# A wave-attention and mixture-of-experts layer on one core: routing's first chunk inside the last attention unit, pad rows in pairs, and a reordered wave projection with warm-up matmuls

## The chip, the cores and the metric

One NeuronCore of a Trainium2 chip runs the whole layer in one launch. The metric is the device time of one execution in microseconds, the median of several executions. The engines are PE (TensorE: matmuls and transposes), PEld (its weight loads), DVE (VectorE), ACT (ScalarE), POOL (GpSimd) and SP (SyncE, which here only issues transfers).

## The reference

The input is x of 4 x 1024 tokens with 256 channels, float32. Four steps follow each other.

```
wave:   wp = silu(x @ w_wave + b_wave)            -> freq, phase, decay (mean over 8 heads)
        q  = silu(x @ w_query + b_query)          -> score slope per head, q . key_weight
        33 sample positions per token, softmax, envelope, weighted sum of x at those positions
        gate (two small matmuls), @ w_out, silu;  x = layernorm(x + out)
msa:    x = x + softmax(q k^T / 4) v @ w_proj     (16 heads of 16, per batch of 1024 tokens)
moe:    z = layernorm(x) * w + b;  logits = z @ gate_w + gate_b;  expert = argmax (8 experts)
        x = layernorm(x + x2 + gelu(z @ w1[e]) @ w2[e])
```

The routing step sorts the 4096 tokens by expert into regions of a scratch tensor `routed`, so that the expert step can take them 128 rows at a time. Where an expert's region does not end on a multiple of 128, rows of zeros with an index beyond the last token fill it up (pad rows).

## The kernel before, in words

The program is a row of blocks. In a block every engine has its own list of instructions, the lists meet only in semaphores, and a barrier of all engines closes the block. Every list is written by hand; no scheduler moves anything.

- **constants** (L116 to L127): POOL makes the identity matrix `ident`, DVE casts it to `identb`. A block of its own, so its barrier stands before the first load.
- **project_waves** (L260 to L454): for each batch b of 1024 tokens, PE transposes x (`turn`, 16 transposes, `pw_pT`, L379), ACT and DVE copy the result to SBUF (`evacuate`, L338, L339, L426), PE multiplies it by the wave and query weights (`project`, `pw_pW`, L388), DVE adds the biases (`bias_add`, `pw_pre`, L410), ACT takes silu (`activate`, L346) and two tanh (`squash`), DVE sums query times key weight (`scores`, L416 and L421). Between these DVE works out the sampling grid of a batch: `locate`, `spots`, `within`, `counts`, `extremes` (L204 to L257). PE's `project` waits for all five loads on ACT's queue (`w_in`), and `project(b)` waits for `bias_add(b-1)`, since both use one PSUM tile. `activate(b)` waits for `qkd`, the end of `scores(b-1)`.
- **wave_sampling**, **gate_and_project**: not touched.
- **attention** (L1481 to L1763): 32 units of two heads, in 8 steps each. A step computes four score tiles (`at_pst`, L1714), ACT takes their exponential (L1616), PE multiplies the step before by v (`at_pacc`, L1724, `values`). The maxima of the next unit are computed in the same steps (`at_pmx`, L1695, three PSUM banks), so the last unit has none. After its last step PE transposes the sum back (`turn_out`, L1706), DVE normalises (L1655, L1661) and SP stores it (L1567). In that unit SP already loads routing's first chunk of the attention's result Y and of the residual y0 (L1595, L1596, tiles `first_y`, `first_y0`).
- **project_and_route** (L1781 to L2129): the tokens in chunks, seven of 512 and two of 256. `rounds()` runs three chunks at once: in round i PE does `project(i)` (L2092), `gate(i-2)` (L2125), `turn(i+1)` (L2083), `turn_n(i-1)` (L2102), `count(i-2)` (L2113 to L2116). ACT copies the transpose (`turn_out`, L1921, tile `pg_yT`), scales (L1928), takes the root (L1936) and normalises into `pg_rows` (L1944). DVE adds the residual (`add`, L2002), takes statistics (`spread`), picks expert and slot (`route_chunk`, `place_chunk`), and keeps the residual (`keep`, L2033). POOL scatters the rows, one indirect transfer for each 128 tokens (L1904). There is one buffer `yc` for Y: SP loads chunk i (L1845) once `turn(i-1)` is done, which is in round i-2; y0 has two buffers (L1848, after `keep(i-2)`). The eight pad transfers (L1840, 258 KB each) stand at i = 2. After the last chunk DVE works out the table of tiles (L2053 to L2070); SP waits for it, reads the first tile's expert, loads that expert's `w1` (L1852), waits for all scatters and loads the first tile's rows (L1857).
- **experts** (L2133 to L2295): 39 tiles of 128 rows, each 16 products with w1 (L2281), gelu, 8 products with w2 (L2291), and the last layernorm.

A float32 matmul stands as two records in the trace: 16 products are x32 there, 8 are x16. Transposes are one record each.

Of the kernel before, what the change touches and what calls it, by code (L numbers as in the profile page):

```python
# [11 lines left out]
P = 128  # L12
# [43 lines left out]
def build(nc, io, dr):  # L56

    with ExitStack() as top:
# [15 lines left out]
        constants(nc, sem, ident, identb)  # L74
# [3 lines left out]
        with ExitStack() as wave:  # L78
# [7 lines left out]
            with ExitStack() as ctx:  # L86
                project_waves(nc, sem, lambda *a: sb(ctx, *a), lambda *a: ps(ctx, *a), io, ident, grid)
# [7 lines left out]
        yn, y_out = [sb(top, f"at_yn{i}", [P, 8, 2, 2 * DK]) for i in range(2)], [sem(f"at_y_out{i}") for i in range(2)]  # L95
        with ExitStack() as both:
# [3 lines left out]
            with ExitStack() as ctx:  # L100
                attention(nc, sem, lambda *a: sb(ctx, *a), lambda *a: ps(ctx, *a), io, dr, ident, w2, w_in, proj_loads, projs_in,
                          first_in, first_loaded, yn, y_out, att)
# [3 lines left out]
        with ExitStack() as ctx:  # L106
            project_and_route(nc, sem, lambda *a: sb(ctx, *a), lambda *a: ps(ctx, *a), io, dr, ident, projs, projs_in, expert, at, first_in, first_loaded,
# [3 lines left out]


def constants(nc, sem, ident, identb):

    zeroed, made = sem("ident_zeroed"), sem("ident_made")
    with nc.Block() as block:  # L116
        @block.gpsimd
        def _(pool):
            nc.gpsimd.memset(ident[:], 0.0).then_inc(zeroed, 1)
            pool.wait_ge(zeroed, 1)  # L120
            nc.gpsimd.affine_select(out=ident[:], in_=ident[:], compare_op=ALU.not_equal, fill=1.0, base=0,
                                    pattern=[[-1, P]], channel_multiplier=1).then_inc(made, 1)

        @block.vector
        def _(dve):
            dve.wait_ge(made, 1)
            nc.vector.tensor_copy(identb[:], ident[:])  # L127
# [132 lines left out]
def project_waves(nc, sem, sb, ps, io, ident, grid):  # L260
# [13 lines left out]
    w_in, x_in = sem("wave_w_in"), [sem(f"wave_x_in{i}") for i in range(2)]  # L274
# [3 lines left out]
    MADE = 9  # L278
    biased, silued, tanhed, qprod, qkd = (sem("wave_" + n) for n in ("biased", "silued", "tanhed", "qk_products", "qk_summed"))
# [7 lines left out]
    with nc.Block() as block:  # L287
# [10 lines left out]
        def _(pool):  # L298
            g = nc.gpsimd
            near = ident[:, 0:2 * TILES].unsqueeze(1).to_broadcast([P, REACH, 2 * TILES])  # L300
# [14 lines left out]
            g.memset(grid.rows[:, grid.EDGE + L:2 * grid.EDGE + L], grid.OUTSIDE).then_inc(made, 1)  # L315
            pool.wait_ge(made, MADE - 1)
# [10 lines left out]
        def _(a):  # L327
            a.dma_start(w[:, :, 0:3 * WH], io["L0_attn_w_wave"].rearrange("(k p) n -> p k n", p=P)).then_inc(w_in, 16)
            a.dma_start(w[:, :, 3 * WH:NW], io["L0_attn_w_query"].rearrange("(k p) n -> p k n", p=P)).then_inc(w_in, 16)
            a.dma_start(bias[:, 0:3 * WH], row(io["L0_attn_b_wave"], 3 * WH)).then_inc(w_in, 16)  # L330
            a.dma_start(bias[:, 3 * WH:NW], row(io["L0_attn_b_query"], WH * POS)).then_inc(w_in, 16)
            a.dma_start(kw[:], row(io["L0_attn_key_weight"], POS)).then_inc(w_in, 16)
# [20 lines left out]

            nc.scalar.activation(warm[:, 0:1], ident[:, 0:1], ACT.Silu)
# [13 lines left out]
        def _(pe):  # L368
# [34 lines left out]
        def _(dve):  # L403
# [24 lines left out]
            c = Chain(dve, grid.nd)  # L428
            evacuate(0)
            dve.wait_ge(w_in, 5 * 16)  # L430
# [5 lines left out]
            dve.wait_ge(qkd, 1)  # L436
# [14 lines left out]
            bias_add(3)  # L451
            grid.extremes(v, c, 1)
# [545 lines left out]

# [1337 lines left out]
```

## Time and profile before

| | us |
|---|---|
| median of 3 runs | 1659.06 |
| lowest, highest | 1658.22, 1660.64 |
| profiled execution, its own time | 1656.7 |
| its span in the trace | 1654.9 |
| PE busy | 1539.9 (93%) |
| DVE busy | 1329.6 (80%) |
| ACT busy | 1012.4 (61%) |
| mean granted TensorE clock | 0.976 |

| stretch of the span, by its first and last work | us |
|---|---|
| constants and project_waves | 0.3 to 49.1 |
| wave_sampling, gate_and_project, attention | 49.6 to 1273.8 |
| project_and_route | 1274.4 to 1359.7 |
| experts | 1361.0 to the end |

The rows are read from one profiled execution. It took 1656.7 us, 1.8 more than its span and 2.4 less than the median of the three timed runs. A timeline row gives start, duration, engine, line, operation, output and input; equal instructions that follow each other stand in one row with their count. In square brackets is the time for which the engine stood idle ahead of it, and what ended that.

### The profile page before, as it was taken

What the parts mean: (1) busy time and instruction counts of PE and PEld (TensorE: products, weight loads), DVE (VectorE), ACT (ScalarE), POOL (GpSimd) and SP (SyncE); (2) the same over time, 40 slices, a digit from 0 to 9 for tenths busy, and PEclk for the clock granted to TensorE, in tenths of its full rate; (3) what the DMA queues carried; (4) which work ended last, traced back from release to release, by engine and by line L of the source; (5) the groups of instructions that cost most, each with busy time, mean ns of one, the idle gap of its engine ahead of it and who ended that gap; (6) DMA issues with size and microseconds to landing.
All of it is one profiled execution on the core that took longest, in us unless ns stands there. A gap on an engine that the chain in (4) does not pass through costs nothing. (4 is left out here: it accounts for less than half of the span.)

```text
span 1654.9 us, 29306 instructions
## 1 busy us (share of the span) xinstructions
PE 1539.9 (93%) x10078; PEld 837.9 (51%) x10078; DVE 1329.6 (80%) x3006; ACT 1012.4 (61%) x1745; POOL 196.0 (12%) x372
## 2 busy tenths in 40 slices
PE   7688999979998999999999999999997859999997
PEld 6465656656553222222222222222222858999996
DVE  5899999846888889888988898889880767777773
ACT  2599999935446777777777777777776532222221
POOL 3011111131110000000000000000000351222222
PEclk9799999999999999999999999999999979999999
DMA  3300110026847322232233222212202766666661
GB/s 108 89 8 14 50 43 21 14 96 218 265 167 197 71 59 55 69 71 54 51 70 71 60 52 71 72 49 56 71 21 81 218 223 236 209 211 210 204 203 54
DMA packets 159154, 172.22 MB, mean 104 GB/s; under 512 B 72912, under 2 KB 118992, under 8 KB 159008
## 3 DMA queue, kind: packets, MB, share of 16 engines
q1 hardware_dynamic: 153600, 156.60, 32.8%
q0 software_dynamic: 4432, 13.50, 2.1%
q8 instruction: 82, 1.34, 0.4%
q14 instruction: 64, 0.52, 0.1%
q10 hardware_dynamic: 976, 0.24, 0.1%
HBM read 120.73 MB, written 49.23 MB: 103 GB/s over the span
## 5 line engine op out<-in xcount | busy, mean ns | idle before, releaser
L1629 DVE TENSOR_REDUCE at_mx<-at_pmx 128x1 f32<-128x512 f32 x980 | 618.0, 681 | 57.8 <-PE at_pmx L1695 56.8
L1616 ACT ACTIVATE at_p<-at_pst 128x512 f32<-128x512 f32 x1024 | 533.2, 603 | 209.8 <-PE at_pst L1714 209.6
L1695 PE MATMUL at_pmx<-at_k,at_q 96*128 96x512 bf16 x980 | 374.7, 383 | 0.0
L1714 PE MATMUL at_pst<-at_q,at_k 99*128 99x512 bf16 x1024 | 346.6, 380 | 4.9 <-ACT at_p L1616 2.6
L1724 PE MATMUL at_pacc<-at_p,at_v 128*32 128x512 f32 x2048 | 272.8, 604 | 0.9 <-ACT at_p L1616 0.7
L1695 PEld LDWEIGHTS at_pmx<-at_k,at_q 96*128 96x128 bf16 x980 | 95.3, 97 | 239.1 <-DVE at_mx L1629 180.0
L1714 PEld LDWEIGHTS at_pst<-at_q,at_k 99*128 99x128 bf16 x1024 | 98.9, 98 | 156.7 <-ACT at_p L1616 92.2
L873 PE MATMUL ws_pA<-ident,ws_A 128*128 128x128 f32 x1088 | 148.6, 283 | 25.6 <-ACT ws_A L655 24.2
L2226 ACT ACTIVATE ex_hT<-ex_pH 128x1024 f32<-128x1024 f32 x39 | 39.9, 1024 | 202.4 <-PE ex_pH L2281 202.4
L873 PEld LDWEIGHTS ws_pA<-ident,ws_A 128*128 128x128 f32 x1088 | 119.8, 143 | 84.3 <-ACT ws_A L655 41.8
L2241 DVE STREAM_TRANSPOSE ex_zr<-ex_row 32x64 f32<-32x64 f32 x608 | 143.2, 235 | 17.9 <-DMA ex_row<-scratch_routed 10.0
L2281 PE MATMUL ex_pH<-ex_zT,ex_w 128*128 128x128 f32 x1248 | 147.8, 277 | 2.9 <-ACT ex_zT L2219 2.9
L2281 PEld LDWEIGHTS ex_pH<-ex_zT,ex_w 128*128 128x128 f32 x1248 | 147.3, 194 | 5.4 <-issue 3.4
L2291 PE MATMUL ex_pY<-w,ex_hT 128*128 x624 | 141.2, 379 | 0.7 <-DVE ex_x L2251 0.7
L2291 PEld LDWEIGHTS ex_pY<-w,ex_hT 128*128 128x128 f32 x624 | 115.6, 190 | 15.2 <-issue 1.1
L655 ACT ACTIVATE ws_A<-ws_steps,par_beta,par_alpha 128x672 f32<-128x672 bf16 (+2 forms) x128 | 100.0, 857 | 2.9 <-issue 2.3
L655 ACT ACTIVATE ws_A<-lent_steps,par_beta,par_alpha 128x672 f32<-128x672 bf16 (+2 forms) x128 | 100.2, 855 | 1.7 <-issue 1.7
L777 DVE TENSOR_TENSOR ws_AT<-ws_pA,ws_hitT 128x768 f32<-128x768 f32 (+2 forms) x96 | 89.8, 952 | 9.6 <-PE ws_pA L873 9.2
L777 DVE TENSOR_TENSOR ws_AT<-ws_pA,lent_hits 128x768 f32<-128x768 f32 (+2 forms) x96 | 90.4, 949 | 8.1 <-PE ws_pA L873 7.8
L1867 POOL MEMSET pg_eps<- 128x1 f32 x1 | 0.1, 104 | 783.4 <-POOLq L1510 783.4
L1724 PEld LDWEIGHTS at_pacc<-at_p,at_v 128*32 128x32 f32 x2048 | 40.8, 108 | 99.3 <-ACT at_p L1616 79.7
L1383 PE MATMUL gp_pQ<-gp_zT,gp_wqkv 128*128 128x512 f32 x128 | 60.9, 602 | 0.0
(271 smaller groups left out, 1568.7 us busy)
## 6 DMA issues: line engine op xcount, KB each, us to landing
ex_w<-in_L_ffn_w SPq DMA_DIRECT2D x39, 1024.0 KB, 5.4
at_q<-scratch_qs SPq DMA_DIRECT2D x192, 64.0 KB, 2.8
at_k<-scratch_ks SPq DMA_DIRECT2D x192, 64.0 KB, 2.9
ex_row<-scratch_routed SPq DMA_DIRECT2D x39, 258.0 KB, 5.0
scratch_v<-gp_v SPq DMA_DIRECT2D x8, 1024.0 KB, 6.9
at_v<-scratch_v SPq DMA_DIRECT2D x32, 256.0 KB, 3.7
w<-in_L_ffn_w SPq DMA_DIRECT2D x16, 512.0 KB, 4.6
scratch_qs<-gp_split SPq DMA_DIRECT2D x16, 384.0 KB, 3.2
```

The costliest lines, as they stand in the source:

```text
L655: nc.scalar.activation(A[:, h % QUAD, cols(g, r)], KB[g][:, cols(g, r)], ACT.Exp, bias=par["beta"][:, t, h], scale=par["alpha"][:, t, h]). ...
L777: v.tensor_tensor(AT[h // QUAD][:, home(h, m[0]):home(h, m[-1]) + 1, :].rearrange("p s l -> p (s l)"), p[:, 0:len(m) * P], mask, ALU.mult) ...
L873: last = nc.tensor.transpose(p[:, to], a, ident[:])
L1383: last = nc.tensor.matmul(pQ[q % 3][:], wqkv[:, k, q * P:(q + 1) * P], zT[:, k, :], start=(k == 0), stop=(k == KC - 1))
L1616: a.activation(pt[k // 2 % 4][:, k % 2, :], pst[bank(w, k)][:], ACT.Exp).then_inc(exped, 1)
L1629: v.reduce_max(mx[u % 2][:, m // 2, m % 2:m % 2 + 1], pmx[bank(w, m)][:], AX.X).then_inc(red, 1)
L1695: nc.tensor.matmul(pmx[bank(w, m)][:], qst[u][0:ROWS, h, nt * P:(nt + 1) * P], kst[u][0:ROWS, h, kh * HALF:(kh + 1) * HALF], start=True, s ...
L1714: nc.tensor.matmul(pst[bank(w, k)][:], kst[u][:, h, t * P:(t + 1) * P], qst[u][:, h, p * HALF:(p + 1) * HALF], start=True, stop=True).then ...
L1724: last = nc.tensor.matmul(pacc[at:at + 2 * DK, :], vst[u][:, s, h, :], pt[(2 * s + p) % 4][:, h, :], start=(s == 0), stop=(s == BT - 1))
L2241: last = v.transpose(zr[j % 2][c * Q:(c + 1) * Q, :, q * Q:(q + 1) * Q], z[q * Q:(q + 1) * Q, :, c * Q:(c + 1) * Q])
L2281: last = nc.tensor.matmul(pH[:, c, :], w1[j % WBUFS][:, k, c * P:(c + 1) * P], zT[:, k, :], start=(k == 0), stop=(k == KC - 1))
L2291: last = nc.tensor.matmul(pY[:], hT[j % 2][:, c, :], w2[:, c, bass.ds(e, 1), :], start=(c == 0), stop=(c == HC - 1))
```

## The change

It has five parts.

1. **The block of constants is gone.** POOL makes `ident` at the head of project_waves, and whoever reads it waits for a semaphore (`diagonal`). SP's and ACT's loads there wait for nothing.
2. **The wave projection is reordered.** `project` waits for the two weight loads alone; the biases and the key weight have a semaphore of their own, on which DVE waits. `bias_add(1)` stands ahead of `extremes(0)`, `bias_add(2)` ahead of `locate(1)`, and `activate(b)` waits for the products of `scores(b-1)` (`qprod`) only. PE gets nine matmuls ahead of the first transposes and seven between `turn(1)` and `turn(2)` (`unread`, 104 columns, written to columns of `pW` that nobody reads).
3. **Routing's chunk 0 moves into attention's last unit**: its transposes behind steps 1 to 4, its copies (DVE, two of 512 columns) behind DVE's last step, its projection behind steps 6 and 7 and around the last `values`, in the banks of the maxima. DVE adds the residual at the block's end. SP loads Y's chunk 1 there too. Routing starts with `turn(1)` and with an activation that loads ACT's table for the root.
4. **Pad rows in pairs**: two transfers after y0's load at i = 3, 4, 5 and 6, in place of eight at i = 2.
5. **w1 of the first tile is loaded without the table**: the table is made so that the first tile always belongs to expert 0 (one more DVE instruction), and SP loads `w1[0]` right after the last y0 load.

```diff
-        constants(nc, sem, ident, identb)
...
+            g.memset(ident[:], 0.0).then_inc(zeroed, 1)
+            pool.wait_ge(zeroed, 1)
+            g.affine_select(out=ident[:], in_=ident[:], compare_op=ALU.not_equal, fill=1.0, base=0,
+                            pattern=[[-1, P]], channel_multiplier=1).then_inc(diagonal, 1)
...
                 if b:
-                    a.wait_ge(qkd, b)
+                    a.wait_ge(qprod, b)
...
+            def unread(n):
+
+                for _ in range(n):
+                    nc.tensor.matmul(pW[:, 0, 0, NW:C], ident[:], ident[:, 0:C - NW], start=True, stop=True)
+
+            pe.wait_ge(diagonal, 1)
+            unread(WARMING)
             turn(0)
-            pe.wait_ge(w_in, 5 * 16)
+            pe.wait_ge(w_in, 2 * 16)
             project(0)
             turn(1)
+            pe.wait_ge(biased, 1)
+            unread(WAITING)
             turn(2)
...
             grid.counts(v, c, 0)
+            bias_add(1)
+            dve.wait_ge(qkd, 1)
             grid.extremes(v, c, 0)
-            bias_add(1)
             scores(1)
+            bias_add(2)
             dve.wait_ge(tanhed, 4)
             grid.locate(v, c, 1)
-            bias_add(2)
             scores(2)
...
+            sp.dma_start(first.yc[:], tokens(dr["Y"], 0)).then_inc(first.y_in, 16)
+            sp.dma_start(first.y0[:], tokens(dr["y0"], 0)).then_inc(first.y0_in[0], 16)
+            sp.wait_ge(first.turned, 1)
+            sp.dma_start(first.yc[:], tokens(dr["Y"], 1)).then_inc(first.y_in, 16)
...
             normalise(UNITS - 1, UNITS // RING - 1, RING - 1)
+            dve.wait_ge(first.outed, 1)
+            dve.wait_ge(first.y0_in[0], 16)
+            for n in range(2):
+                ins = v.tensor_tensor(first.x2[:, 2 * n:2 * n + 2, :], pO[n], first.y0[:, 2 * n:2 * n + 2, :], ALU.add)
+            ins.then_inc(first.added, 1)
...
+                    if final and TURNED <= s < TURNED + first.T:
+                        turn_first(s - TURNED)
+                    if final and s >= PROJECTED:
+                        project_first(s - PROJECTED)
...
             units(unit)
+            project_first(BT - PROJECTED)
             values(UNITS - 1, RING - 1, BT - 1)
+            project_first(BT - PROJECTED + 1)
...
-                if i == 2:
-                    sp.wait_ge(consts, CONSTS)
-                    for e in range(E):
-                        sp.dma_start(dr["routed"][e * REGION:e * REGION + P, :], padrow[:]).then_inc(pads_sent, 16)
...
+                if PADS <= i < PADS + E // 2:
+                    sp.wait_ge(consts, CONSTS)
+                    for e in range((i - PADS) * 2, (i - PADS) * 2 + 2):
+                        sp.dma_start(dr["routed"][e * REGION:e * REGION + P, :], padrow[:]).then_inc(pads_sent, 16)
...
+            sp.dma_start(w1[0][:], io["L0_ffn_w1"][0, :, :].rearrange("(k p) n -> p k n", p=P)).then_inc(w1_in[0], 16)
             sp.wait_ge(table, TABLE)
-            e = sp.value_load(expert[0:1, :], min_val=0, max_val=E - 1)
...
-            turn_out(0)
+            a.activation(warm[:], ident[:, 0:1], ACT.Sqrt)
...
-            turn(0)
             for i, prev, pp in rounds():
-                if i is not None:
+                if i:
                     project(i)
```

The order on PE at the end of attention and the head of routing, first of the kernel before. `at_pst` are score tiles, `at_pacc` the products with v, `at_pm` the transposes back, `pg_pY` and `pg_pO` routing's transposes and projection.

```order
L1714 MATMUL at_pst<-at_q,at_k 128x512 x4
L1724 MATMUL at_pacc<-at_p,at_v 32x512 x4
L1714 MATMUL at_pst<-at_q,at_k 128x512
L1724 MATMUL at_pacc<-at_p,at_v 32x512 x4
L1706 MATMUL at_pm<-ident,at_oe 128x128 x4
L1510 UNCONDITIONAL_BRANCH
L2073 UNCONDITIONAL_BRANCH
L2083 MATMUL pg_pY<-ident,first_y 128x128 x8
L2092 MATMUL pg_pO<-pg_wproj,pg_yT 128x256 x8
L2083 MATMUL pg_pY<-ident,first_y 128x128 x8
```

And of the kernel after, from step 6 of the last unit on. `at_pmx<-pg_wproj` is the projection of chunk 0.

```order
L1744 MATMUL at_pst<-at_q,at_k 128x512
L1772 MATMUL at_pmx<-pg_wproj,at_first_yT 128x256 x2
L1744 MATMUL at_pst<-at_q,at_k 128x512 x3
L1754 MATMUL at_pacc<-at_p,at_v 32x512 x4
L1744 MATMUL at_pst<-at_q,at_k 128x512
L1772 MATMUL at_pmx<-pg_wproj,at_first_yT 128x256 x4
L1754 MATMUL at_pacc<-at_p,at_v 32x512 x4
L1772 MATMUL at_pmx<-pg_wproj,at_first_yT 128x256 x2
L1736 MATMUL at_pm<-ident,at_oe 128x128 x4
L1526 UNCONDITIONAL_BRANCH
L2135 UNCONDITIONAL_BRANCH
L2145 MATMUL pg_pY<-ident,first_y 128x128 x8
```

Eight products of the projection now stand between score tiles and around the last product with v; behind the barrier only `turn(1)` is left of what stood ahead of `project(1)`.

SP's transfers at the head of routing, before:

```order
L1845 DMA first_y<-scratch_Y 128x4x256
L1848 DMA pg_y<-scratch_y 128x4x256
L1840 DMA scratch_routed<-pg_padrow 128x516 x8
L1845 DMA first_y<-scratch_Y 128x4x256
L1848 DMA first_y<-scratch_y 128x4x256
```

And after:

```order
L1902 DMA first_y<-scratch_Y 128x4x256
L1905 DMA pg_y<-scratch_y 128x4x256
L1909 DMA scratch_routed<-pg_padrow 128x516 x2
L1902 DMA first_y<-scratch_Y 128x4x256
L1905 DMA first_y<-scratch_y 128x4x256
L1909 DMA scratch_routed<-pg_padrow 128x516 x2
L1902 DMA first_y<-scratch_Y 128x4x256
```

The eight pad transfers no longer stand ahead of chunk 2's load; each of chunks 4 to 7 has a pair ahead of its load.

## Rows read from the trace of the kernel before

**Rows 1.** Timeline of project_waves: start us, us, engine, line, operation.

```profile
0.80 0.21 POOL L119 MEMSET ident<- 128x128 f32 x1 [0.29 <-POOLq L2325]
...
2.06 0.45 SPq L290 DMA_DIRECT2D pw_x<-in_L_attn_x  x1
...
11.65 6.05 PE L388 MATMUL pw_pW<-pw_w,pw_xT 128*128 128x152 f32 x32 [1.41 <-DVE pw_xT L426]
...
17.81 1.43 DVE L410 TENSOR_TENSOR pw_pre<-pw_pW,pw_bias 128x1216 f32<-128x1216 f32 x1 [6.31 <-PE pw_pW L388]
...
21.53 3.30 PE L379 MATMUL pw_pT<-ident,pw_x 128*128 128x128 f32 x16 [2.09 <-ACT pw_xT L339]
...
29.11 1.91 PE L379 MATMUL pw_pT<-ident,pw_x 128*128 128x128 f32 x16
...
30.85 4.34 PE L388 MATMUL pw_pW<-pw_w,pw_xT 128*128 128x152 f32 x32
...
32.02 1.23 DVE L416 TENSOR_TENSOR pw_prod<-pw_act,pw_kw 128x1024 f32<-128x1024 f32 x1 [1.28 <-ACT pw_act L346]
...
47.91 1.22 DVE L421 TENSOR_REDUCE ws_A<-pw_prod 128x64 f32<-128x1024 f32 x1
```

**Rows 2.** Windows: us, busy PE, PEld, DVE, ACT, POOL, PEclk, DMA share, GB/s.

```profile
27.61:29.31 1.70, 1.70 (x15) 1.70 (x15) 1.59 (x9) 0.00 (x0) 0.00 (x0) 1.00 0.00 0
...
1305.00:1309.00 4.00, 4.00 (x36) 3.92 (x35) 3.06 (x9) 2.13 (x5) 3.39 (x3) 1.00 0.48 144
1309.00:1313.00 4.00, 4.00 (x33) 3.59 (x31) 3.79 (x17) 3.14 (x7) 2.27 (x3) 1.00 1.03 302
```

**Rows 3.** Timeline of PE in attention's last unit, its last steps.

```profile
1267.21 0.39 PE L1714 MATMUL at_pst<-at_q,at_k 99*128 99x512 bf16 x1 [0.26 <-ACT at_p L1616]
...
1269.61 1.06 PE L1724 MATMUL at_pacc<-at_p,at_v 128*32 128x512 f32 x8 [0.69 <-ACT at_p L1616]
1271.47 0.63 PE L1706 MATMUL at_pm<-ident,at_oe 128*128 128x128 f32 x4 [0.80 <-ACT at_oe L1609]
```

**Rows 4.** Timeline of attention's end, and of an addition of 512 columns.

```profile
1272.43 0.42 DVE L1661 TENSOR_TENSOR at_yn<-at_pm,at_rden 128x256 f32<-128x256 f32 x1
1272.88 0.91 SPq L1567 DMA_DIRECT2D scratch_Y<-at_yn  x2
...
1336.52 0.68 DVE L2002 TENSOR_TENSOR lent_x<-pg_pO,pg_y 128x512 f32<-128x512 f32 x1
```

**Rows 5.** Chain that ended last, through routing: start us, us, what.

```profile
1274.56 1.93 PE pg_pY L2083 x8
...
1276.56 1.02 ACT pg_yT L1921
...
1277.63 5.58 PE pg_pO L2092 x16
...
1284.11 7.07 DMA first_y<-scratch_Y
...
1294.52 3.79 PE pg_pO L2092 x16
...
1315.82 7.59 DMA first_y<-scratch_Y
```

**Rows 6.** Timeline of PE: the transposes behind that last load.

```profile
1323.45 1.09 PE L2083 MATMUL pg_pY<-ident,first_y 128*128 128x128 f32 x8 [1.16 <-DMA first_y<-scratch_Y]
```

**Rows 7.** Transfers of routing: KB each, median us from issue to landing.

```profile
scratch_routed<-pg_padrow SPq DMA_DIRECT2D x8, 258.0 KB, 6.9
...
first_y<-scratch_Y SPq DMA_DIRECT2D x3, 512.0 KB, 5.8
...
pg_y<-scratch_y SPq DMA_DIRECT2D x1, 256.0 KB, 3.2
```

**Rows 8.** Chain, routing's end: start us, us, what.

```profile
1355.89 3.49 DMA scratch_routed<-pg_rows,pg_slot
...
1359.67 4.58 DMA ex_row<-scratch_routed
```

More of the change, by code:

```diff
@@ L257, in extremes, with project_waves @@
         v.tensor_tensor(self.reach[:, t, :], self.over(self.gain, u, self.NK), self.along(self.ks, u), ALU.mult).then_inc(self.ranges, 1)
-def project_waves(nc, sem, sb, ps, io, ident, grid):
+def project_waves(nc, sem, sb, ps, io, ident, identb, grid):
     xb = [sb(f"pw_x{i}", [P, BT, C]) for i in range(2)]
@@ L1480, in _, with attention @@
                     n += 1
-def attention(nc, sem, sb, ps, io, dr, ident, w2, w_in, later, later_in, first_in, first_loaded, yn, y_out, att):
+def attention(nc, sem, sb, ps, io, dr, ident, w2, w_in, later, later_in, first, yn, y_out, att):
     UNITS = B * H // 2
@@ L1683, in _ @@
             units(unit)
+            dve.wait_ge(later_in, 16 * len(later))
+            dve.wait_ge(first.turned, 1)
+            for k in range(KC):
+                ins = v.tensor_copy(yT[:, k, :], pY[k][:])
+            ins.then_inc(first.yTd, 1)
             invert(UNITS - 1)
             normalise(UNITS - 1, UNITS // RING - 1, RING - 1)
+            dve.wait_ge(first.outed, 1)
[3 more added lines that the diff above has]
+            ins.then_inc(first.added, 1)
         @block.tensor
@@ L1726, in values, with turn_first, project_first @@
                 last.then_inc(pv, 1)
+            def turn_first(t):
+                if t == 0:
+                    pe.wait_ge(first.y_in, 16)
+                    pe.wait_ge(red, UNITS * MAXIMA)
+                for k in range(KC):
+                    last = nc.tensor.transpose(pY[k][:, t * P:(t + 1) * P], first.yc[:, t, k * P:(k + 1) * P], ident[:])
+                if t == first.T - 1:
+                    last.then_inc(first.turned, 1)
+            def project_first(t):
+                if t == 0:
+                    pe.wait_ge(later_in, 16 * len(later))
+                    pe.wait_ge(first.yTd, 1)
+                for k in range(KC):
+                    last = nc.tensor.matmul(pO[t // 2][:, t % 2, :], yT[:, k, t * P:(t + 1) * P], first.wp[:, k, :],
+                                            start=(k == 0), stop=(k == KC - 1))
+                if t == first.T - 1:
+                    last.then_inc(first.outed, 1)
             def unit(w, i, u):
-                first = w == 0
+                final = w == UNITS - 1
+                begun = w == 0
                 pe.wait_ge(rows_in, (w + 1) * 48)
@@ L1744, in unit @@
                             if s == TURN and turns(w):
-                                if not first:
+                                if not begun:
                                     pe.wait_ge(yd, w)
@@ L1749, in unit @@
                                 values(w, u, s - 1)
[L1750 removed]
+                            elif not begun:
                                 values(w - 1, (u - 1) % RING, BT - 1)
[L1752 removed]
+                            if s == 2 and not begun:
                                 if turns(w - 1):
```

84 lines of the change are left out of this document (44 added, 40 removed).

## The prediction

> **What bounds the kernel now.** By the table above PE is busy for 93% of the span. The change leaves the long middle alone, 49.6 to some 1250 us, so I looked at the two stretches that it touches, first with the chain of work that ended last, then with the timeline. At the front [rows 1] DVE ends last: its last sum ends at 47.91 + 1.22 = 49.13 us. The reader is to see that it stands idle on the way: 6.31 us for the first product, then three times 1.27 or 1.28, twice for ACT's silu (one row stands for both) and once for the fourth product. In routing [rows 5] the chain runs over PE but for two loads of Y: 7.07 us for chunk 2, while PE waits, and 7.59 for chunk 6. At the end it runs over the last scatter and the load of the first tile's rows [rows 8].
>
> **Parts 1 and 2, the front.** (a) SP's first load goes out at 2.06 us, behind the barrier of the constants; POOL's first own work is at 0.80 [rows 1]. Loads that wait for nothing should go out then, say at 0.85: **-1.2**. Their landings shift with them, and so does what waits for x. Bounds: 0, if something else gates the queue, and -1.3.
>
> (b) The first product takes 6.05 us, the third 4.34 for the same 32 records; sixteen transposes take 3.30 in one place, behind an idle time of 2.09, and 1.91 in another [rows 1]. So PE is at its lower level (1.2 GHz) at the start and again from 21.5 us. The nine warm-up matmuls fill the time from 1.6 us, when `ident` is there, until x lands near 5; PE has nothing else then, so they cost nothing. If the clock is up when the first product starts, it takes 4.34: **-1.7**. Bounds: 0, and -2.6 with half of the first transposes fast as well. The seven matmuls behind `turn(1)` fill part of the idle 2.09 and end before ACT's copy does: no cost. Their gain is that the second product is done when DVE, now early, asks for it.
>
> (c) DVE's three waits go: behind each bias addition now stands grid work. The piece that covers the first, `extremes(0)`, takes 1.70 from its first to its last instruction [rows 2], more than silu's 1.28; the pieces at the other two are of that size. That is 3.8. What comes late next is the third product: PE must do `turn(3)` and `project(2)`, 1.91 + 4.34 [rows 1], behind the second, and DVE waits some 0.7 for it. Net **-3.1**. Bounds: -1.5, if the clock is low for the second and fourth product (each 1.7 longer, of which about half would show), and -3.8.
>
> Front: -1.2 - 1.7 - 3.1 = **-6.0**, from -2.5 to -7.5. POOL's and ACT's work there has slack and shifts along.
>
> **Part 3, the last unit and routing's head.** It adds eight transposes in steps 1 to 4, two a step at 0.12 us (1.91 for 16, [rows 1]). PE waits 0.26 us for an exponential in such a step [rows 3], which covers them. The projection stands in four pieces; all four take 3.79 at the high clock [rows 5], 0.95 each. The first is in a step with a wait of 0.26 and some overlap: +0.5. The second and third stand together ahead of the last product with v, where PE waits 0.69, and the score tile ahead of it leaves 0.15: 1.90 - 0.84, +1.0. The fourth covers the 0.80 that PE waits for ACT's copy [rows 3]: +0.1. Sum +1.6. DVE then adds 2 x 0.68 behind its normalisation and ends at 1272.85 + 1.36 = 1274.2, where SP's stores ended the block at 1272.88 + 0.91 = 1273.8 [rows 4]: +0.4. Together **+2.0**. Bounds: +1.2, with all waits used, and +5.0, with no piece covered.
>
> What it takes out: from routing's first transpose, 1274.56, to the third projection, 1294.52, there are 19.96 us [rows 5]. This stretch will hold `turn(1)` 1.93, its copy 1.02, `project(1)` 5.58, `turn(2)` 0.96, its copy 1.02 (over `turn_n(0)`), and 0.2 of hand-overs: 10.7. Chunk 2's load is not on this path any more: it is issued 2 us into the block, beside y0 alone, and has 6.6 us, where the later loads took 5.8 in the median [rows 7]. So **-9.3**. I keep the low clock's 5.58 there, since PE idles over the barrier as before. Bound on the high side: -12.2, with a high clock; on the low side -7.5, if that load is late by 1.8.
>
> **Part 4, the pads.** Behind the third projection PE waits once, 1.16 us for chunk 6's load [rows 6]; that load took 7.59 [rows 5], so PE leaves a load 6.4. Now a pair of pads, 2 x 258 KB, goes out ahead of each of four loads. At the 302 GB/s of a full window [rows 2] a pair is 1.75 us of transfer. Chunk 4's load runs before the scatters, with room (the DMA share in the first window of scatters is 0.48, [rows 2]). Chunk 5's has 0.6 to spare by the median of 5.8: 1.2 late. Chunk 6's gets 1.75 later. Chunk 7 is half the size. That is 3.0 if nothing falls into idle time of the DMA engines. I take **+2.0**, from 0 to +6.
>
> The Trainium skill, "DMA: Bandwidth & Descriptors", section "Queues, rings and completion order", says that on each DMA engine the descriptors of one queue are consumed in ring order. The trace agrees as far as it goes, with 7.07 us for the load behind eight pads. That rule speaks against this part; its full form is rival C.
>
> **Part 5, the first tile.** Its rows took 4.58 us to land beside 1 MB of w1 [rows 8]; a load of the same size took 3.2 elsewhere in routing [rows 7]. With w1 long there: **-1.3**, from 0 to -2. The added DVE instruction is off the path, where the chain names the last scatter [rows 8], not the table. w1 now travels beside the scatters of chunks 5 to 8; only the last one's landing counts, and w1 is through before that.
>
> **Sum.** -6.0 + 2.0 - 9.3 + 2.0 - 1.3 = **-12.6**. On the profiled execution that is 1654.9 - 12.6 = 1642.3 of span, 1644.1 of time. It lay 2.4 below the median of the timed runs; against the median, 1659.06 - 12.6 = **1646.5**.
>
> **The rivals.** *A, the clock does not answer.* It stays low through the first product and falls again in the waits. Then the front brings 1.2 + 1.5 = 2.7, and the sum is -9.3: 1649.8. For it: at 21.5 us an idle time of 2.09 was enough for slow transposes [rows 1]. Against it: with the warm-up PE has nearly no pause from 1.6 us to the end of the first transposes.
> The Trainium skill, "TensorE: Matmul & The Clock Gate", Part 1, says that the low clock is the default and activity lifts it, and warns that the number of slow matmuls varies from run to run. By that, term (b) can lie anywhere between its bounds; the one trace cannot show it.
>
> *B, the clock is up at routing's head*, because PE works closer to the barrier. Then the -9.3 is -12.2 and the sum -15.5: 1643.6. Against it: the idle time over the barrier is no shorter than before.
>
> *C, each pair holds the load behind it for its own landing.* This one ends slower. A pad takes 6.9 us to land [rows 7] and is issued some 2.4 ahead of the load. If the load starts only then, it lands 6.9 - 2.4 + 5.8 = 10.3 after its issue, 3.9 late, and four of them 15.6. After waits of this length PE's clock is low, and sixteen transposes take 1.4 longer [rows 1]: 4 x 1.4 more. That is 21.2 in place of 2.0, +6.6: 1665.7. It decides from 3.65 us a pair on, where the other parts' 14.6 are gone. Against it: chunk 2's load stood behind eight pads and took 7.07, not 6.9 + 3.
>
> *D, the unit gives nothing away.* Every piece put into the last unit comes out in full at its end: +5.0 in place of +2.0, sum -9.6: 1649.5. It would mean that the pacing of ACT and PE leaves no room, against the 0.26, 0.69 and 0.80 of [rows 3]. This is also how the change would fail to do what it says.
>
> **How the numbers follow.** Forecast, within 1644.5 and 1648.5: 0.50. A: 0.15. B: 0.12. D, or the pads at their bound of +6 (1650.5): 0.15. C: 0.04. A and the pads' bound together (1653.8), or worse but not slower: 0.04. The predicted time is the likeliest case's. The range reaches to 1642.0 for B with a better front, and to 1652.0 for A, for D and for the pads' bound. A measurement of this kernel can tell about 0.2%, 3.3 us, from no change. All cases but C and a part of the last are faster than that: faster 0.94, same 0.03, slower 0.03.
>
> **What would show each step.** The first load issued near 0.9 us; the first product 4.3 us long, or 6; DVE's last sum in project_waves ending near 43 us, with no idle 1.28 behind a bias addition; attention's last unit 1.6 longer on PE; 10.7 us from routing's first transpose to the projection of chunk 2, with no wait for a load; waits of PE for `first_y` of 3 us in all between chunks 4 and 7; the first tile's rows landing in 3.3 us. The prediction is wrong above all if loads of Y come late in more than two rounds, or if the front ends later than 46 us.

## The result, and the profile after

| | before | after |
|---|---|---|
| median | 1658.64 (1656.60 to 1660.64, 4 runs) | 1647.55 (1646.81 to 1649.47, 4 runs) |
| profiled execution's span | 1654.9 | 1644.8 |
| mean granted TensorE clock | 0.976 | 0.976 |

The ratio is 0.9935, 95% interval 0.9918 to 0.9952. The forecast was 1646.5. Two further comparisons of the same two kernels gave 0.9929 and 0.9938 (below), so by the ratios the change is worth 10.3 to 11.8 us, 11.0 in the mean of the three; the sum had said 12.6. A ratio is not the quotient of two medians of this document and can lie up to 0.0009 away from it: by the medians alone the three differences are 11.1, 10.8 and 8.9 us, 10.2 in the mean.

The wave projection after the change, timeline rows as in [rows 1] (start us, us, engine, line, operation, idle time ahead and what ended it):

```profile
0.80 0.45 SPq L275 DMA_DIRECT2D pw_x<-in_L_attn_x  x1
...
1.58 4.17 PE L386 MATMUL pw_pW<-ident 128*128 128x104 f32 x18 [1.58 <-POOL ident L287]
...
9.97 4.37 PE L379 MATMUL pw_pW<-pw_w,pw_xT 128*128 128x152 f32 x32 [1.41 <-DVE pw_xT L426]
...
30.27 1.42 DVE L410 TENSOR_TENSOR pw_pre<-pw_pW,pw_bias 128x1216 f32<-128x1216 f32 x1 [0.51 <-PE pw_pW L379]
...
41.93 1.22 DVE L421 TENSOR_REDUCE ws_A<-pw_prod 128x64 f32<-128x1024 f32 x1
```

The first load goes out at 0.80 instead of 2.06, the first product takes 4.37 instead of 6.05, no bias addition has an idle 1.28 behind it, and DVE's last sum ends at 43.15 instead of 49.13. A new wait has come up in between, of DVE for POOL:

```profile
36.42 0.30 DVE L216 TENSOR_SCALAR ws_A<-ws_A 128x264 bf16<-128x264 uint16 x1 [0.69 <-POOL ws_A L209]
```

PE in the last unit, the counterpart of [rows 3]. `at_pmx<-pg_wproj` is chunk 0's projection, `at_pst` a score tile, `at_pacc` a product with v:

```profile
1263.48 0.39 PE L1744 MATMUL at_pst<-at_q,at_k 99*128 99x512 bf16 x1 [0.26 <-ACT at_p L1636]
...
1265.02 1.03 PE L1772 MATMUL at_pmx<-pg_wproj,at_first_yT 128*128 128x256 f32 x4
...
1267.85 1.89 PE L1772 MATMUL at_pmx<-pg_wproj,at_first_yT 128*128 128x256 f32 x8
1269.68 1.06 PE L1754 MATMUL at_pacc<-at_p,at_v 128*32 128x512 f32 x8
1270.67 1.13 PE L1772 MATMUL at_pmx<-pg_wproj,at_first_yT 128*128 128x256 f32 x4
1271.64 0.60 PE L1736 MATMUL at_pm<-ident,at_oe 128*128 128x128 f32 x4
1274.70 1.06 PE L2145 MATMUL pg_pY<-ident,first_y 128*128 128x128 f32 x8 [2.46 <-PEq L1526]
```

The waits of 0.69 and 0.80 are gone, filled by the projection. The last row is routing's first transposes; they take 1.06, where [rows 5] has 1.93.

The chain of waits through routing, the counterpart of [rows 5, 8] (start us, us, what):

```profile
1276.96 3.72 PE pg_pO L2154 x16
...
1282.65 3.72 PE pg_pO L2154 x16
...
1296.45 7.86 DMA first_y<-scratch_Y
...
1345.68 2.96 DMA scratch_routed<-pg_rows,pg_slot
...
1348.94 2.65 DMA ex_row<-scratch_routed
```

The first row is chunk 1's projection, the second chunk 2's. Chunk 2's load is no longer on the chain. Chunk 5's load is, and PE waits for it and is then at its lower level (1.2 GHz) for a while. The timeline shows it in the 1.52 us of eight transposes, and the granted clock is 0.58 in the window from 1304.36 to 1307.79:

```profile
1304.36 1.52 PE L2145 MATMUL pg_pY<-ident,first_y 128*128 128x128 f32 x8 [1.43 <-DMA first_y<-scratch_Y]
```

The two profiles differ by 10.1 us of span. By stretch: the front is 6.0 shorter, the last unit 1.5 longer, routing from its first transpose to its last projection 10.3 shorter, its tail 2.5 shorter. That is 17.3. But 4.6 us came back between the start of wave sampling and the last unit, and 2.6 in the experts, in code that the change does not touch. What those 7.2 are was the first question.

### The profile page after: what moved, and what is told of

Its sections match the earlier page's. It is cut to its first block and busy times, and to the rows that moved or that the text cites. A ratio compares the mean times of both kernels' runs of the same rounds, so it can differ in the third digit from the quotient of the medians.

```text
span 1644.8 us, 29359 instructions
## 1 busy us (share of the span) xinstructions
PE 1544.4 (94%) x10110; PEld 841.1 (51%) x10110; DVE 1331.6 (81%) x3010; ACT 1011.4 (61%) x1745; POOL 197.1 (12%) x372
```

## Experiments

All times are medians; each ratio is to runs of the kernel before on the same chip. Their median is 1662.08 us for the two kernels without an edit, the front alone and the kernel without warm-up; 1662.28 for the pads in one burst, the late w1 and the first runs of the two kernels with pads in attention; 1661.13 for the last four. The changed kernel did not run on the second of these chips, so those four are compared with it by their ratios only.

### The same two kernels again

One theory: the length of the untouched middle is a matter of where the clock falls in that execution. Its rival: the middle really gives part of the front's gain back. Both kernels ran again without an edit.

> The kernel before, unchanged, for a second trace. Theory M (the middle's time depends on where TensorE's low clock falls): against the first trace of this kernel, which had 1222.9 us from wave_sampling's first DVE sum at 49.95 to the first transpose back in attention's last unit, this trace has a time that differs by 1 to 5 us, and every step of the difference falls in a stretch where one of the two traces shows a granted clock of 0.50. Theory S (the change itself lengthened the middle by 4.6 us): this trace repeats the first one within 0.5 us there. Time: the same, ratio 1.000.

> The changed kernel, unchanged, for a second trace and a tighter ratio. Theory M: the middle (same two instructions) is anywhere from 1222 to 1228 us, not 1227.5 again but by chance; the front ends at 43.2 us again, and the stretch from routing's first transpose to chunk 2's projection is 8.0 us if the clock stays up over the barrier and 10.7 if it doesn't. Theory S: 1227.5 again within 0.5. Ratio to before 0.9935 within 0.001.

**Measured:** 1661.42, ratio 0.9996 [0.9981, 1.0012]; and 1651.30, ratio 0.9929 [0.9906, 0.9952]. The middle, from the first work of wave sampling to the transposes back of the unit before the last, was 1206.1 us in the first trace of the kernel before and 1211.8 in this one; that of the changed kernel was 1210.75 and 1210.94. (The two expectations measure one unit further and give 1222.9 and 1227.5 us; by the timeline that stretch is 1221.5 and 1227.7.) Windows over the middle, of the kernel before in its two traces, then of two later experiments whose middle is the shortest and the longest of all (columns as in [rows 2]: us, busy PE, PEld, DVE, ACT, POOL, PEclk, DMA share, GB/s):

```profile
49.95:1256.06 1206.11, 1150.98 (x7443) 483.62 (x7443) 1046.38 (x1904) 874.27 (x1514) 72.43 (x151) 0.99 0.28 77
```

```profile
48.24:1260.04 1211.80, 1154.85 (x7444) 484.69 (x7444) 1046.82 (x1904) 874.43 (x1514) 72.75 (x151) 0.98 0.28 77
```

```profile
43.43:1249.07 1205.64, 1150.88 (x7446) 484.00 (x7446) 1045.77 (x1904) 874.01 (x1514) 72.67 (x151) 0.99 0.28 77
```

```profile
43.60:1258.11 1214.51, 1159.90 (x7445) 489.25 (x7446) 1047.07 (x1904) 874.36 (x1514) 73.91 (x153) 0.98 0.29 77
```

DVE and ACT are busy for the same time in all four, to 1.3 us. PE's busy time goes from 1150.9 to 1159.9 for the same work, and the span of the stretch goes with it, 1205.6 to 1214.5. Where the difference arises can be read from the two traces of the kernel before. Cut at the same instructions, they differ in three stretches. First those of the first trace:

```profile
189.49:249.84 60.35, 54.62 (x572) 35.66 (x571) 57.76 (x92) 57.77 (x77) 10.14 (x24) 1.00 0.12 34
249.84:289.77 39.93, 35.86 (x401) 23.93 (x398) 38.53 (x61) 36.40 (x49) 5.20 (x12) 1.00 0.06 22
...
489.89:529.40 39.51, 34.77 (x143) 16.14 (x145) 33.51 (x61) 22.13 (x40) 1.05 (x1) 0.96 0.67 192
```

Then the same work in the second:

```profile
187.78:249.28 61.50, 55.91 (x572) 36.65 (x571) 57.84 (x92) 57.77 (x77) 10.36 (x24) 0.97 0.12 34
249.28:290.35 41.07, 37.14 (x401) 24.92 (x398) 38.77 (x62) 36.40 (x49) 5.22 (x12) 0.96 0.06 21
...
490.66:533.32 42.66, 37.92 (x143) 17.01 (x145) 33.61 (x61) 22.24 (x40) 1.06 (x1) 0.88 0.66 181
```

**What follows.** These three are 1.15, 1.14 and 3.15 us longer, and in each the granted clock is lower: 0.97, 0.96 and 0.88 in place of 1.00, 1.00 and 0.96. The rest of the middle differs by 0.25 us. So within one kernel the middle's length is a matter of how long its clock was low, and the first trace of the kernel before was a short one. The total of 5.7 is a little outside the 1 to 5 that was expected. The changed kernel's two traces agree over the middle to 0.2 us, which by itself would fit the rival as well; but the 4.6 us between the first two profiles need no loss to the change, and the timed halves below say that there is none.

The 2.6 us of the experts are of the same kind. Their second product takes 3.81 us in one group of traces and 5.44 in the other, here before and after:

```profile
1373.71 3.81 PE L2281 MATMUL ex_pH<-ex_zT,ex_w 128*128 128x128 f32 x32 [1.92 <-ACT ex_zT L2219]
```

```profile
1361.99 5.44 PE L2342 MATMUL ex_pH<-ex_zT,ex_w 128*128 128x128 f32 x32 [1.92 <-ACT ex_zT L2280]
```

The granted clock is 1.00 from 1374 to 1378 in the trace before and 0.69 from 1362 to 1367.5 in the trace after. The seven traces with 3.81 have 290.3 to 290.7 us of experts, the seven with 5.44 have 292.4 to 293.2, and kernels with the old and the new routing stand in both groups.

### One half alone

Parts 1 and 2 (no block of constants, the reordered wave projection) without the rest. Against the changed kernel:

```diff
-            project_first(BT - PROJECTED)
             values(UNITS - 1, RING - 1, BT - 1)
-            project_first(BT - PROJECTED + 1)
...
+            turn(0)
             for i, prev, pp in rounds():
-                if i:
+                if i is not None:
                     project(i)
...
```

And parts 3 to 5 without those, again against the changed kernel:

```diff
+        constants(nc, sem, ident, identb)
...
-            unread(WARMING)
             turn(0)
-            pe.wait_ge(w_in, 2 * 16)
+            pe.wait_ge(w_in, 5 * 16)
             project(0)
             turn(1)
-            pe.wait_ge(biased, 1)
-            unread(WAITING)
             turn(2)
...
```

> The kernel before with parts 1 and 2 alone (no block of constants, reordered wave projection, warm-up matmuls). The front's last DVE sum ends at 43.2 us, 6.0 earlier than before. Theory M: the total gains 6.0 plus or minus what the clock does in the middle, ratio 0.9964, anywhere from 0.994 to 0.999. Theory S: it gains 1.4 (6.0 less 4.6), ratio 0.9992. Routing is as before: the load of chunk 2 takes about 7 us behind eight pads.

> Parts 1 and 2 alone, once more, since the first measurement gave -2.0 with an interval from -4.3 to +0.3 while the traces show the front 4.1 to 5.7 us shorter. Additive theory: -5, ratio 0.997, within 0.9955 and 0.9985. Given-back theory: -2 or less again, 0.9988 to 1.000. The stretch from the start of wave sampling to the last unit is 1205.6 to 1213.8 us in the ten traces of any of these kernels; the additive theory expects this one in that range with no lean.

> The kernel before with parts 3, 4 and 5 of the change alone: the constants' block and the wave projection stay as they were. Additive theory (both halves pay in full, and the middle's length is chance): the stage table of the traces so far gives last unit +1.5, routing from its first transpose to the last projection -5.9 (means of four and three traces), its tail -2.3, together -6.7 of 1662: ratio 0.996, within 0.9945 and 0.9975. Theory that the front's gain is given back in the middle: then the whole 0.7% of the change must come from here, ratio 0.993 to 0.994. In the trace the last sum of the wave projection ends near 49 us as before, and the last unit is 17.24 us long.

> The changed kernel itself on the chip of this comparison: 0.993 as twice before. Additive theory: its gain is the sum of those of routing alone and of the front alone, to within the three intervals. Given-back theory: it equals that of routing alone.

**Measured.**

| kernel | us | ratio | 95% |
|---|---|---|---|
| front alone | 1659.27 | 0.9988 | 0.9974, 1.0002 |
| front alone, again | 1657.30 | 0.9972 | 0.9962, 0.9981 |
| routing alone | 1657.00 | 0.9968 | 0.9952, 0.9983 |
| both, the changed kernel | 1652.28 | 0.9938 | 0.9918, 0.9958 |

The first measurement of the front alone spoke for the given-back theory: 2.0 us in ratio, where its trace shows a front more than 4 us shorter. The last three ran beside each other on one chip, and there the halves add up: 0.28% and 0.32% make 0.60%, and the whole gives 0.62%. By the medians of the same runs it is 3.8 and 4.1 us, and 8.9 for the whole. Under the given-back theory routing alone had to give the whole 0.6 to 0.7%; its interval ends at 0.48%. What stays open is whether the front brings the 5.3 us of the traces or the 4.7 [3.1, 6.3] of the better measurement; the two agree within that interval.

### Without the warm-up

```diff
-    WARMING, WAITING = 9, 7
+    WARMING, WAITING = 0, 0
```

> The changed kernel without the nine and the seven warm-up matmuls (nothing else differs; they write columns that nobody reads). If they bought the clock, as forecast: the first transposes take some 3.5 and the first product 5 to 6 us instead of 4.37, the last DVE sum of the front ends 2 to 3.5 us later than 43.15, and the total is 2 to 3 us longer than the changed kernel's, unless the middle's clock hides it. If the rival holds (the clock rises whatever is done): the front ends at 43.2 again.

**Measured:** 1654.72, ratio 0.9950 [0.9932, 0.9968], beside 0.9929 with the warm-up. PE's timeline at the front of this kernel:

```profile
5.05 3.83 PE L370 MATMUL pw_pT<-ident,pw_x 128*128 128x128 f32 x16 [5.05 <-DMA pw_x<-in_L_attn_x]
10.29 7.40 PE L379 MATMUL pw_pW<-pw_w,pw_xT 128*128 128x152 f32 x32 [1.41 <-DVE pw_xT L426]
```

The first product takes 7.40 us, and wave sampling starts at 47.30 instead of 43.49. Windows over the product, up to the point where its pace changes and behind it (columns as in [rows 2]):

```profile
10.29:16.24 5.95, 5.95 (x23) 5.95 (x24) 0.00 (x0) 0.00 (x0) 2.19 (x2) 1.00 0.54 176
16.24:17.69 1.45, 1.45 (x12) 1.45 (x12) 0.00 (x0) 0.00 (x0) 0.00 (x0) 1.00 0.00 0
```

Up to 16.24 us one record starts each 0.25 us, behind it each 0.13. So even this product ran at the lower level for three quarters of its records only. The PEclk column reads 1.00 in both windows: at the head of the program the level has to be read from the pace of the records. Over all traces: in the four without a warm-up the product took 4.40, 6.05, 6.17 and 7.40; in the ten with one it took 4.37 each time. **What follows.** Against the traces with the sixteen matmuls, whose results nobody reads, this one starts wave sampling 3.2 to 3.9 us later. In another trace without them the product took 4.40, so they gain little in some executions; the four have a mean of 6.0, 1.6 more than 4.37. They take the chance out of this place. Rival A, the clock that does not answer, is out. The product was expected at 5 to 6 us and was slower; the front is 3.3 us later than the 43.15 of the first trace after, within the 2 to 3.5. The two intervals of the timed runs overlap, so the timed 3.4 alone would not settle it; the row does. No run has the nine without the seven.

### Pads in one burst, and w1 behind the table

```diff
+                if i == 2:
+                    sp.wait_ge(consts, CONSTS)
+                    for e in range(E):
+                        sp.dma_start(dr["routed"][e * REGION:e * REGION + P, :], padrow[:]).then_inc(pads_sent, 16)
-                if PADS <= i < PADS + E // 2:
...
```

> The changed kernel with part 4 undone: all eight pad transfers again ahead of chunk 2's load. Theory P (pairs of pads make one or two later loads of Y late, 1.4 us in all, and PE's clock falls behind the wait, together some 3 us from chunk 2's projection to chunk 7's): that stretch falls from the 40.1 and 41.7 us of the changed kernel's two traces to 38.6, as in the kernel before. But chunk 2's load now lands some 4 us later behind the pads, so PE waits for it ahead of its transposes: the stretch from routing's first transpose to chunk 2's projection grows from 8.0 or 10.7 to 14 to 16.5. Net 2 to 4 us slower than the changed kernel. Rival (pads in pairs cost as much as they save): the same time.

```diff
-            sp.dma_start(w1[0][:], io["L0_ffn_w1"][0, :, :].rearrange("(k p) n -> p k n", p=P)).then_inc(w1_in[0], 16)
             sp.wait_ge(table, TABLE)
+            sp.dma_start(w1[0][:], io["L0_ffn_w1"][0, :, :].rearrange("(k p) n -> p k n", p=P)).then_inc(w1_in[0], 16)
```

> The changed kernel with the first w1 load behind the table again (still expert 0's, so the instruction that SP needs to read the expert's number is not there). Theory R (the early load takes 1 MB out of the way of the first tile's rows): the rows take 4.6 to 4.8 us to land instead of 2.6, the total is 1.9 to 2.2 longer than the changed kernel's by the trace's routing end. Rival: w1's early load is what makes the late loads of Y late; then PE's waits for Y fall as well and the total is the same.

**Measured:** 1653.68, ratio 0.9957 [0.9943, 0.9972]; and 1653.90, ratio 0.9955 [0.9939, 0.9971]. SP and PE of the first, around chunk 2's load:

```profile
1276.43 5.02 SPq L1900 DMA_DIRECT2D scratch_routed<-pg_padrow  x8
1281.49 0.65 SPq L1906 DMA_DIRECT2D first_y<-scratch_Y  x1
```

```profile
1287.18 1.18 PE L2145 MATMUL pg_pY<-ident,first_y 128*128 128x128 f32 x8 [4.14 <-DMA first_y<-scratch_Y]
```

**What follows.** Eight pads in a burst hold SP's queue for 5.02 us, and then the load still takes 5.64 to land. With chunk 0 gone from routing there is nothing left to cover that: PE waits 4.14, and the stretch from the first transpose to chunk 2's projection is 15.4 us instead of some 9.8. Behind it no load is late, and the rest is 46.0 instead of some 49.7. So the pairs are a trade, 5.6 won for 3.7 paid; the timed ratios, 0.9957 against 0.9934 in the mean, have the same sign, with intervals that overlap. With w1 behind the table, its load starts 1.0 us after the last scatter's and runs beside that and beside the first tile's rows:

```profile
1346.17 3.87 DMA scratch_routed<-pg_rows,pg_slot
1347.18 0.37 SPq L1913 DMA_DIRECT2D ex_w<-in_L_ffn_w  x1
1350.34 3.18 DMA ex_row<-scratch_routed
```

The two landings take 3.87 and 3.18 where the profile after has 2.96 and 2.65, and the tail is 25.63 us instead of 23.6. The rows were expected to take 4.6 to 4.8, as before the change, and did not. This run does not bring the old order back whole: without the instruction that reads the expert's number, w1 goes out 3.16 us ahead of the rows, where it was 1.95 (1357.72 and 1359.67) before. The rival, that the early w1 makes the loads of Y late, is out: chunks 5 and 6 are 1.52 and 1.39 us late here too. The timed interval overlaps that of the changed kernel, so the early w1 is worth some 2 us by one trace and not more certainly than that.

### No pads beside the loads

The pad rows are made in attention's block and sent by SP in the last unit, behind chunk 0's loads.

```diff
+            sp.wait_ge(first.pads_made, 2)
+            for e in range(E):
+                sp.dma_start(dr["routed"][e * REGION:e * REGION + P, :], first.padrow[:]).then_inc(first.pads_sent, 16)
             sp.wait_ge(first.turned, 1)
...
-                if PADS <= i < PADS + E // 2:
...
```

> The changed kernel with the eight pads issued in attention's last unit, behind y0's first load, where the DMA engines are idle (their row is made by POOL at attention's start). Theory P: no load of Y behind a pad any more; PE's waits for Y are 0 to 1.2 us in all, the stretch from chunk 2's projection to chunk 7's falls to 38.6 us, and the total is 2 to 3 us below the changed kernel's. Attention's end must not move: SP is done with the pads some 6 us before the last result is to be stored. Rival (the waits come from the scatters, whatever the pads do): the waits for chunks 5 and 6 stay at 1 to 2 us and nothing is gained.

The same, with each of the four pieces of chunk 0's projection in a place of its own: one behind step 5, one behind step 6, and one on either side of the last product with v:

```diff
-                    if final and s >= PROJECTED:
-                        project_first(s - PROJECTED)
+                    if final and s in (5, 6):
+                        project_first(s - 5)
...
-            project_first(BT - PROJECTED)
+            project_first(2)
             values(UNITS - 1, RING - 1, BT - 1)
-            project_first(BT - PROJECTED + 1)
+            project_first(3)
```

> As the one before, and the four pieces of chunk 0's projection each in a place of its own: behind steps 5 and 6 and on either side of the last product with v. In the changed kernel the last unit, from the transposes back of the unit before to its own, takes 17.24 us against 15.76. If a piece costs what it is over the wait in its step, as forecast (+0.5, +1.0, +0.1), this one gives +0.5, +0.5, +0.1, +0.1, so 17.0 at most and 16.9 at best, 0.3 less. If pieces are free in a step of their own: 16.2.

> Pad rows sent in the last unit and chunk 0's projection in one piece behind each of steps 5 and 6 and around the last product with v, once more, beside the changed kernel on one chip. If it is better, its ratio is 0.990 to 0.992 against the changed kernel's 0.993. The last unit is 16.8 us long instead of 17.24, and of the loads of Y those of chunks 5 and 6 still come late by some tenths to 1 us, since the scatters and not the pads are beside them.

**Measured:** 1648.79, ratio 0.9915 [0.9893, 0.9938]; 1646.48, ratio 0.9905 [0.9881, 0.9929]; and again, on the last chip, 1650.32, ratio 0.9931 [0.9917, 0.9944], where the changed kernel had 0.9938. The window in which chunk 5's load runs, of the changed kernel and of the one without pads beside it:

```profile
1297.00:1305.00 8.00, 6.57 (x54) 6.06 (x53) 6.88 (x27) 4.18 (x8) 5.35 (x6) 0.99 1.05 338
```

```profile
1302.00:1310.00 8.00, 7.61 (x64) 7.09 (x63) 6.91 (x27) 4.74 (x9) 5.00 (x5) 1.00 0.83 237
```

And the two late loads that are left in the chain of the kernel of 0.9905:

```profile
1294.20 6.53 DMA first_y<-scratch_Y
...
1301.90 7.45 DMA first_y<-scratch_Y
```

**What follows.** Without pads chunk 5's load takes 6.5 to 6.8 us instead of 7.4 to 8.2 (7.86 in the first trace after), or is on time. Chunk 6's is on time in one of the three traces and takes 7.45 and 7.80 us in the others; with pairs it takes 7.04 to 8.99 in the four traces where PE waits for it, and 7.59 in [rows 5], where the pads are long through. So a load can be late with no pad near it, and the pads add about 1 us to chunk 5's. What makes it late then was not tested: the scatters run beside it, but no run takes them away. The rest of routing takes 47.4, 47.6 and 47.8 us in these three traces, against 47.7 to 50.9 in the six with pairs. The last unit is 16.8 instead of 17.24. The stretch from chunk 2's projection to chunk 7's, for which 38.6 was expected, is 37.7, 40.0 and 40.2 us. By the traces these versions are some 2 us better than the changed kernel, by the two comparisons of the last one 2.6 in the mean. Beside the changed kernel on one chip it was 0.9931 against 0.9938, 1.2 us, where 0.990 to 0.992 had been expected, and the intervals overlap each time. That they beat it is not shown.

## The prediction, point by point

The stretches of all traces, in us. "Old" are traces in which the stretch is as in the kernel before, "new" as in the changed kernel; each number is a difference of two starts in the timeline. The last unit is taken from the first of the four transposes back of the unit before to the last of its own four, and "the last projection" is the start of its last record. The kernels with pads in attention stand in the first row alone.

| stretch | old | mean | new | mean | forecast | measured |
|---|---|---|---|---|---|---|
| start to wave sampling's first work | 49.95, 48.24, 48.83 | 49.0 | 43.97, 43.49, 43.55, 44.13, 43.41, 44.11, 43.43, 43.68, 43.51, 43.60 | 43.7 | -6.0 | -5.3 |
| last unit | 15.76, each | 15.8 | 17.24, each | 17.2 | +2.0 | +1.5 |
| first transpose to chunk 2's projection | 19.75, 17.07, 17.60, 20.84 | 18.8 | 7.96, 10.72, 10.73, 9.42, 10.55, 9.65 | 9.8 | -9.3 | -9.0 |
| from there to the last projection | 46.26, 46.93, 46.19, 48.76 | 47.0 | 47.74, 49.36, 49.96, 50.78, 50.94, 49.25 | 49.7 | +2.0 | +2.6 |
| from there to the experts | 23.73, 26.81, 26.28, 25.15 | 25.5 | 21.24, 24.39, 24.83, 24.41, 23.10 | 23.6 | -1.3 | -1.9 |

The measured column sums to -12.1, the forecast to -12.6; the timed runs say -11.0 by their ratios, from -10.3 to -11.8, and -10.2 by their medians.

- **Right: what bounds each end.** DVE's last sum ended the front, and the chain through routing ran where it was expected to.
- **The front, -6.0.** (a) came out at 1.26 and the product of (b) at 1.68 in that trace. The first product also starts 1.68 earlier, 0.42 more than the load: the first transposes take 3.02 us instead of 3.94, which (b) had as a bound. They start at 5.54, where the kernel without warm-up starts them at 5.05, so the nine matmuls did hold them up by 0.49, though the sum had them free. The first bias addition is thus 3.35 earlier, and 2.63 of the 5.98 are left for (c), where 3.1 was said. The three waits of 3.83 in all went, and the named successor came, the third product, late by 0.51 where 0.7 was said. The sum had nothing for the second, DVE's 0.69 for POOL's share of the sampling positions: that POOL's work has slack there was wrong. 3.83 less 0.51 and 0.69 is 2.63. What the sum did not see either is that (b) starts from a number that is itself a draw: without warm-up matmuls and with the old front the product took 4.40, 6.05 and 6.17 in three traces. The 5.3 of the means is the better size. (The bounds named for the three terms add up to -1.5 and -7.7, not to the -2.5 and -7.5 of the text.)
- **The last unit, +2.0.** The 1.6 on PE was 1.48, and it was 1.48 in every trace that has this unit. The 0.4 for DVE's additions did not appear: the time from the last transposes back to routing's first is 2.73 with them and 2.74 without. In the profile after, SP's stores are issued until 1273.02 + 0.91 = 1273.93 and PE starts 0.77 later, as before (1273.79 and 1274.56); the additions end at 1272.91 + 1.28 = 1274.19, inside those 0.77. The error was to take the end of the issue for the end of the block. Rival D is out: three pieces filled the waits that [rows 3] shows.
- **Routing's head, -9.3.** Built from 10.7 us, which three traces have or nearly have (10.72, 10.73, 10.55). In the first trace after, rival B's case occurred, 7.96 with a product of 3.72 us instead of 5.6. One trace would have had B confirmed; in the other five chunk 1's product took 5.18 to 6.49. The granted clock over it is 1.00 in the first trace after and 0.55 in the second. So B's clock is the exception. The lower side of the difference moved too: the old stretch is 17.1 to 20.8 long by how late chunk 2's load is (waits of 2.32, 0.44, 1.04 and 3.41 us). The forecast's single number sits in the middle of both.
- **The pads, +2.0.** The means give +2.6, within the 0 to +6. Chunk 5's load was 0.67 to 2.03 us late in the six traces, chunk 6's up to 2.56. PE's waits for loads of Y behind chunk 3 come to 1.3 to 3.2 us in the six traces, where 3 was said. The mechanism was half right: a pair adds about 1 us to chunk 5's load, but a load is late without pads too. The sum took 1.75 us of transfer for each pair, which is too much, and left out the low clock behind a late load, which costs as much again: the interval between two projections is 7.43 us when nothing is late and 10.27 around the one wait of 1.43. These two errors offset each other, so that the +2.0 came out near is luck in part.
- **Rival C, the pair's own landing ahead of the load's,** would have had loads of 10.3 us. They took 7.0 to 9.0.
- **The first tile's rows, -1.3.** The rows land in 2.60 to 2.72 us instead of 4.58 to 5.08: -2.1 by itself, at the far bound, so the 3.2 of [rows 7], taken from a load elsewhere in routing, was too high for this one. The late w1 has 3.18 for these rows, so the reason that was given, w1 out of the way, is borne out for some 0.5 us there; the rest of the 2.1 depends on how close ahead of the rows w1 goes out, and no run sets that apart.
- **Missing from the sum: the spread of the profiled execution.** The forecast took 2.4 us between that execution and the median of the timed runs and asked for no more. The middle alone, with nothing changed in it, is 1205.6 to 1214.5 us over the fourteen traces. The kernel before was profiled with a middle of 1206.1, at the short end. That cancels out of a sum of differences, which is why the forecast holds; but it made the two profiles disagree with their own stretches by 7 us.

## What to carry to other kernels

Price a change by the differences of its own stretches, and before comparing two profiles compare the stretches that nothing touched: here their spread is 8.9 us, nearly as large as the effect. Work that is moved into a stretch paced by two engines can go into its waits; here, of 3.8 us of projection and 0.96 of transposes, 1.5 came out. Look also at the engine that was said to have slack: once the waits around it went, POOL was 0.7 us late. A burst of transfers hurt the load behind it through the time that its issue held the queue, 5.02 us; in pairs it cost less there and some in the rounds behind, so look for a stretch with an empty queue before sharing it out.

## What the runs showed of the hardware

- PE's level behind one and the same wait is not fixed. Routing's first transposes in the second trace of the kernel before, where [rows 5] has 1.93 us:

```profile
1278.53 1.22 PE L2083 MATMUL pg_pY<-ident,first_y 128*128 128x128 f32 x8 [2.46 <-PEq L1510]
```

And chunk 1's product in the second trace of the changed kernel, where the first has 3.72:

```profile
1276.67 6.48 PE pg_pO L2154 x16
```

- A product of 32 records takes 4.37 us when all of it runs at 2.4 GHz. The 7.40 of the kernel without warm-up and the 6.05 in the profile before are mixtures of both levels, so the bound of 2.6 for the gain of a warm-up, which went by the 6.05, was no bound: the kernel without one starts wave sampling 3.2 to 3.9 us later than those with it.
- Eight transfers of 258 KB took 5.02 us to issue, a later pair 0.98; the load issued behind them landed 5.64 us later with eight ahead and 7.86 with two ahead and scatters under way.
- The Trainium skill, "TensorE: Matmul & The Clock Gate", Part 1, warns that the number of slow matmuls varies from run to run. The trace agrees: PE's busy time over the same middle is 1150.9 to 1159.9 us.
